# Cross-attention on folded weights in a four-layer Perceiver kernel, with context tiles, weights and normalisations prepared a stage earlier

## The reference, cut to what matters

```
x = x + L2_ffn(layernorm(x))      # 8 experts, top 2, 160 rows kept for each expert, relu
x = x + L3_xattn(layernorm(x), ctx_768, ...)
x = x + L3_attn(layernorm(x), ...)
x = x + L3_ffn(layernorm(x))      # 8 experts, top 2, no row dropped, gelu

def L3_xattn(m1, m2, ...):        # one head; the context has 257 rows of 192 features
    x1 = layernorm(m1, ln1_g, ln1_b);  x2 = layernorm(m2, ln2_g, ln2_b)
    q = x1 @ Wq + bq;  k = x2 @ Wk + bk;  v = x2 @ Wv + bv
    return softmax(q @ k.T * E ** -0.5) @ v @ Wo + bo

def L3_attn(x, ...):              # one head
    q, k, v = x @ Wq.T + bq, x @ Wk.T + bk, x @ Wv.T + bv
    qk = q @ k.T
    theta = 0.5 + 0.2 * sigmoid(qk) + 0.15 * tanh(qk) + 0.1 * relu(qk)
    return (softmax(theta) @ v) @ Wo.T + bo
```

## Time and profile before

| | |
|---|---|
| three runs | 1694.1 us median (1691.71 to 1694.96) |
| the profiled execution | 1691.59 us, span 1689.7 us |
| PE busy | 1527.2 us (90%) |
| DVE busy | 1060.3 us (63%) |
| ACT busy | 830.9 us (49%) |
| POOL busy | 767.7 us (45%) |
| mean granted TensorE clock | 0.96 |
| DMA | 204.52 MB, mean 121 GB/s |

### The profile page before, as it was taken

One profiled execution on the slowest core, in us unless ns is written; L12 is line 12 of the kernel. 1 busy time (PEld: TensorE's weight loads), 2 busy tenths in 40 slices (PEclk: granted clock), 3 DMA queues, 4 the chain that ended last, 5 costly groups with the idle time before them and its releaser, 6 DMA issues. The chain is left out here.

```text
span 1689.7 us, 37134 instructions
## 1 busy us (share of the span) xinstructions
PE 1527.2 (90%) x13507; PEld 1317.3 (78%) x13507; DVE 1060.3 (63%) x2934; ACT 830.9 (49%) x2414; POOL 767.7 (45%) x894
## 2 busy tenths in 40 slices
PE   7999999988888999988999999997769697859998
PEld 6899999856567999976899999964459644649997
DVE  5888888556867788865877777749831142353332
ACT  5766666555336787852766666640014122113332
POOL 7665666353339999943211211228823311113332
PEclk9999999999999999998999999999969988969999
DMA  8655554212013333303533333343056272942221
GB/s 259 199 165 175 172 165 150 99 70 83 1 39 101 132 134 132 134 22 102 187 110 111 130 108 108 126 162 100 0 168 182 45 239 90 360 144 33 39 39 26
DMA packets 127222, 204.52 MB, mean 121 GB/s; under 512 B 21034, under 2 KB 92363, under 8 KB 126659
## 3 DMA queue, kind: packets, MB, share of 16 engines
q1 hardware_dynamic: 119016, 188.83, 34.3%
q0 software_dynamic: 6720, 8.79, 3.2%
q10 hardware_dynamic: 1306, 4.51, 0.8%
HBM read 161.76 MB, written 41.14 MB: 120 GB/s over the span
## 5 line engine op out<-in xcount | busy, mean ns | idle before, releaser
L1074 DVE TENSOR_SCALAR xattn_oT<-banks,xattn_last 128x256 f32<-128x256 f32 x254 | 111.1, 479 | 89.8 <-PE banks L854 89.2
L963 ACT ACTIVATE xattn_probs<-banks,xattn_negmax 128x257 f32<-128x257 f32 x256 | 123.3, 482 | 85.4 <-DVE xattn_negmax L1055 85.2
L968 ACT ACTIVATE xattn_probs<-xattn_probs,xattn_rsum 128x257 f32<-128x257 f32 x256 | 131.3, 513 | 1.4 <-DVE xattn_rsum L1059 1.4
L1351 POOL TENSOR_SCALAR xattn_probs<-xattn_probs,xattn_rsum 128x257 f32<-128x257 f32 x128 | 119.4, 933 | 23.9 <-DVE xattn_rsum L1624 23.1
L974 ACT CAST xattn_probsT_hi<-banks 128x256 fp32r<-128x256 f32 x256 | 94.8, 370 | 57.2 <-PE banks L829 57.2
L1055 DVE TENSOR_REDUCE xattn_negmax<-banks 128x1 f32<-128x257 f32 x256 | 106.2, 415 | 13.4 <-PE banks L820 12.0
L1064 DVE TENSOR_TENSOR xattn_probsT_lo<-banks,xattn_probsT_hi 128x256 fp32r<-128x256 f32 x256 | 105.5, 412 | 11.2 <-ACT xattn_probsT_hi L974 10.2
L765 POOL COPY ctx_stat<-xattn_mv 128x2 f32<-128x2 f32 x32 | 6.0, 187 | 225.0 <-DVE xattn_mv L1088 225.0
L829 PE MATMUL banks<-ident,xattn_probs 128*128 128x128 f32 x512 | 101.6, 281 | 6.2 <-ACT xattn_probs L968 5.7
L816 PE MATMUL banks<-xattn_ctxT,xattn_qk_hi 128*128 128x258 f32 x256 | 93.7, 366 | 0.5 <-DVE xattn_qk L1051 0.5
L715 POOL TENSOR_SCALAR xattn_ctxT<-xattn_rawT 128x514 fp32r<-128x514 f32 x32 | 49.9, 1558 | 88.7 <-issue 82.5
(11 more groups left out here) (516 smaller groups left out, 5093.8 us busy)
## 6 DMA issues: line engine op xcount, KB each, us to landing
xattn_ctxT<-ctx_partsT SPq DMA_DIRECT2D x64, 516.0 KB, 4.1
xattn_ctxN<-ctx_partsN SPq DMA_DIRECT2D x64, 384.0 KB, 4.1
ctx_partsT<-xattn_ctxT SPq DMA_DIRECT2D x32, 516.0 KB, 2.7
moe_w<-in_L_ffn_W SPq DMA_DIRECT2D x16, 1024.0 KB, 12.8
ctx_partsN<-xattn_ctxN SPq DMA_DIRECT2D x32, 384.0 KB, 3.5
moecap_w_early<-in_L_ffn_w SPq DMA_DIRECT2D x10, 1024.0 KB, 10.3
xattn_rawN<-in_ctx SPq DMA_DIRECT2D x32, 192.0 KB, 2.7
...
```

The source lines that it names most:

```text
L963: nc.scalar.activation(probs[:, n % RING, :], SB[n % 2][:, 0:KV], ACT.Exp, bias=negmax[:, n % RING:n % RING + 1], accum_out=psum[:, n % RI ...
L968: nc.scalar.mul(probs[:, n % RING, :], probs[:, n % RING, :], rsum[:, n % RING:n % RING + 1]).then_inc(norm_ready, 1)
L1074: nc.vector.tensor_scalar(oT[k][:, heads, b, :], by_head(out_banks(n)[k][:, k * 2 * P:(k + 1) * 2 * P]), last[:, k, j * PER_TILE + b:j * P ...
L1351: nc.gpsimd.tensor_scalar(probs[:, n % RING, :], probs[:, n % RING, :], rsum[:, n % RING:n % RING + 1], None, ALU.mult).then_inc(norm_read ...
```

## The change

The parameters of the cross-attention are folded: once per run `m` is computed from Wq and Wk, `vo` from Wv and Wo, and the biases are folded alongside. This takes the place of `queries` and of `values`; `project(t)` is then two matmuls for each tile, in every step, and the walk has 12 steps. The folding itself is done by PE and ACT at the end of the capacity stage. Three context tiles of the cross-attention and all weights of the last attention are loaded by SP near the end of the capacity stage; the ring of context tiles has six places; the ring of experts' weights there has three, so that expert 3 and those after it are loaded when `down` of the expert three places earlier is done. The products of weights of the last attention, its folded biases and the first half of its layer norm are computed in the last four steps of the cross-attention; the last attention in turn starts the layer norm of the last expert stage. The tables and gate weights of the last expert stage are loaded a stage sooner, its experts 6 and 7 and its two bias arrays a stage later, behind the border.

```
+class SoftWeights:
+
+
+    LOADS = 8
...
+    def sp(self, sp):
+        for to, m in zip((self.wq, self.wk, self.wv, self.wo), self.drams):
+            sp.dma_start(to[:, :, :], m.rearrange("(c p) n -> p c n", p=P)).then_inc(self.loaded, 16)
+        for n in range(3):
+            sp.dma_start(self.b[:, n * CD:(n + 1) * CD], self.b_drams[n]).then_inc(self.loaded, 16)
+        sp.dma_start(self.bo[:, :], self.bo_dram.partition_broadcast(P)).then_inc(self.loaded, 16)
...
+    def queries_keys(self, pe, bank):
+        pe.wait_ge(self.loaded, 16 * self.LOADS)
+        self.product(bank, self.wq, self.wk).then_inc(self.qk_done, 1)
+
+    def values_out(self, pe, bank):
+        self.product(bank, self.wv, self.wo).then_inc(self.vo_done, 1)
...
+            pe.wait_ge(hw.qk_ready, 1)
             for n in range(2):
-                if soft_theta:
-                    pe.wait_ge(ln.xnT_ready, CD * (n + 1))
-                else:
-                    if n:
-                        ln.turn(pe, 1, LATE)
-                    ln.transposed(pe, n)
+                if n:
+                    ln.turn(pe, 1, LATE)
+                ln.transposed(pe, n)
...
+    RING = 3
...
-            for e in range(cw.EARLY + 1, E):
-                if e >= cw.RING:
-                    sp.wait_ge(down_done, e - cw.RING + 1)
+            for e in range(cw.RING, E):
+                sp.wait_ge(down_done, e - cw.RING + 1)
                 cw.load(sp, e)
+            for t in range(kv.EARLY):
+                kv.load_keys(sp, t)
+                kv.load_rows(sp, t)
+            hw.sp(sp)
...
+                if n == E:
+                    pe.wait_ge(hT_ready, E * FCH)
+                    xw.extra_columns(pe, EXTRA)
+                    xw.values_out(pe, VALUES_OUT)
+            xw.queries_keys(pe, QUERIES_KEYS, BIASES)
...
+            xw.take_extra_columns(act, EXTRA)
+            xw.take_values_out(act, VALUES_OUT)
+            xw.take_queries_keys(act, QUERIES_KEYS, BIASES)
             bring(act, range(1, TILES, 2))
...
         def _(sp):
-            gate.sp(sp)
-            sp.dma_start(token[:, :], d["token_number"]).then_inc(loaded, 16)
-            sp.dma_start(number[:, :], d["number"][0:BLOCKS].partition_broadcast(P)).then_inc(loaded, 16)
-            sp.dma_start(place[:, :], d["number"][1:P + 1].partition_broadcast(P)).then_inc(loaded, 16)
-            sp.dma_start(not_behind[:, :, :], d["not_behind"].partition_broadcast(P)).then_inc(loaded, 16)
-            sp.dma_start(spare[:, :], d["spare"][:, 0:BLOCKS]).then_inc(loaded, 16)
-            sp.dma_start(b1[:, :, :], d["L3_ffn_b1_cols"].rearrange("e p f -> p e f")).then_inc(loaded, 16)
-            sp.dma_start(b2[:, :, :], d["L3_ffn_b2"].partition_broadcast(P)).then_inc(loaded, 16)
+            ew.load(sp, ew.EARLY)
             rows.store(sp, ln, gate, stored, begun)
+            for e in range(ew.EARLY + 1, E):
+                ew.load(sp, e)
+            ew.biases(sp)
...
+    def values_out(self, pe, bank):
+        for of, out in ((slice(0, P), bank[:, 0:D]), (slice(P, self.CTX), bank[0:self.C2, D:2 * D])):
+            for k in range(CD):
+                mm = self.core.nc.tensor.matmul(out, self.wvT[:, k, of], self.wo[:, k, :], start=(k == 0), stop=(k == CD - 1))
+        mm.then_inc(self.vo_done, 1)
...
+    def queries_keys(self, pe, m_bank, b_bank):
+        nc, AUG, K2 = self.core.nc, self.AUG, self.AUG - P
+        pe.wait_ge(self.extra_ready, 2 * CD)
+        pe.wait_ge(self.wide_ready, 3)
+        for c in range(CD):
+            for k in range(CD):
+                nc.tensor.matmul(m_bank[:, c * AUG:(c + 1) * AUG], self.wqT[:, k, c * P:(c + 1) * P], self.wkT[:, k, :],
+                                 start=(k == 0), stop=(k == CD - 1))
+        for of, out in ((slice(0, P), b_bank[:, 0:1]), (slice(P, AUG), b_bank[0:K2, 1:2])):
+            for k in range(CD):
+                nc.tensor.matmul(out, self.wkT[:, k, of], self.bq[:, k:k + 1], start=(k == 0), stop=(k == CD - 1))
+        for k in range(CD):
+            nc.tensor.matmul(b_bank[:, D:2 * D], self.bv_wide[:, k, :], self.wo[:, k, :], start=(k == 0), stop=False)
+        nc.tensor.matmul(b_bank[:, D:2 * D], self.core.ident[:, :], self.bo[:, :], start=False, stop=True).then_inc(self.m_done, 1)
...
+            def project(t):
+                pe.wait_ge(oT_ready, 2 * (t + 1))
+                if t >= 2:
+                    pe.wait_ge(x_done, t - 1)
+                nc.tensor.matmul(Y[t % 2][:, 0:D], oT1[:, t % 2, :], vo1[:, :], start=True, stop=False)
+                nc.tensor.matmul(Y[t % 2][:, 0:D], oT2[:, t % 2, :], vo2[:, :], start=False, stop=True).then_inc(y_done, 1)
...
+            xw.folded(pe)
+            for h in range(2):
+                ln.pe(pe, h)
+                to_context(h)
+            for s in range(STEPS):
                 if s < TILES:
-                    if s < 2:
-                        pe.wait_ge(xT_ready, 2 * CD)
                     scores(s)
-                if s == 0:
-                    queries(1)
-                if s == 1:
-                    to_context(1)
                 if 0 <= s - 1 < TILES:
                     turn_probs(s - 1)
                 if 0 <= s - 3 < TILES:
                     turn_out(s - 3)
-                if s >= 5 and s % 2:
-                    values((s - 5) // 2)
-                if s >= 6 and s % 2 == 0:
-                    project((s - 6) // 2)
+                if 0 <= s - 4 < TILES:
+                    project(s - 4)
                 if 0 <= s - 2 < TILES:
                     probs_ctx(s - 2)
+                if s == QUERIES_KEYS_AT:
+                    pe.wait_ge(scaled_ready, TILES - 1)
+                    hw.queries_keys(pe, QUERIES_KEYS)
+                elif s == FOLD_AT:
+                    pe.wait_ge(scaled_ready, TILES)
+                    hw.fold_biases(pe, FOLD)
+                elif s == VALUES_OUT_AT:
+                    pe.wait_ge(probsT_ready, 2 * TILES)
+                    hw.values_out(pe, VALUES_OUT)
+                elif s == TURN_NEXT_AT:
+                    pe.wait_ge(o_ready, TILES)
+                    nx.turn(pe, 0, NEXT)
...
+                oh = soft_weights(core, until_attn3, ctx)
+                kv = ContextTiles(core, until_kv, ctx, cn)
+                stage_moe_capacity(core, cw, xw, kv, oh)
+            stage_xattn3(core, cn, xw, kv, to_attn3, oh)
+            until_kv.close()
         ew = ExpertWeights(core, ctx)
-        stage_attn3(core, ew)
-        stage_moe(core, ew)
+        stage_attn3(core, oh, to_attn3, to_moe, ew)
+        until_attn3.close()
+        stage_moe(core, ew, to_moe)
...
```

612 lines of the change are left out of this document (306 added, 306 removed).

## The result

The changed kernel takes 1665.5 us in the median of four executions (1659.9 to 1673.1), beside 1693.2 us (1691.7 to 1695.0) for the kernel before. The ratio is 0.985, with a 95% interval of 0.982 to 0.988. The profiled execution took 1663.99 us, its span is 1662.1 us.

A forecast was written before the change was run, and what follows sets the result against it. The prediction took chains of dependent work at stage starts and ends as the bound; 1.7 - 17.3 - 10.1 - 5.7 + 0.7 = -30.7 us from 1691.6 made 1660.9, forecast as 1662 us, range 1653 to 1671.

The forecast's parts named there:

- three signs: Wrong if `up` of experts 3 to 7 waits for DMA, `bring` starts over 3 us late, or first block awaits weights.
- Capacity stage, +1.7: End of the capacity stage: folding matmuls between last `down` and last `turn_y` cost 2.55 us, partly hidden by a 0.77 wait.
- Cost 0: Capacity stage: expert loads through the ring of three, and 23 transfers (5.8 MB) ahead of `bring`, were costed at 0.
- rival of the starving ring: Capacity stage: landings of 15.5 us make five experts wait 6.2 us each, 31 together, giving 1693 us; chance 0.03.
- rival of loads in their way: Capacity stage: loads slow the last experts' additions, giving 1665 us, or keep `bring` waiting, 1668 to 1676; chance 0.12.
- Folding behind `turn_y` at nothing: Capacity stage: about 3.8 us on PE and four ACT copies fit before `bring`, so cost nothing.
- Cross-attention, -17.3: Cross-attention: earlier start, first `turn_probs` at 22.7 us, and full steps of 3.9 us shorten the stage by 17.3 us.
- Pricing the second product by its gap: Cross-attention start: after a 1.5 us PE gap the second product runs at slow clock, 5.3 us instead of 3.7.
- A stretch at half clock in the walk, 0.17: Rival, cross-attention walk: one half-clock stretch costs 5.0 us, giving 1667 us, two 1672; chance 0.17.
- Last attention, -10.1: Last attention: takes 37.4 us where 47.5 stood, starting like the other one-head attention, without waiting for weights.
- Start of the last stage, -5.7 + 0.7: Last expert stage: first gate operation at 9.7 us instead of 15.5 (-5.7), late last expert and biases +0.7.
- late biases: Last expert stage: last expert and biases land 16.1 us after the first gate operation, costing 0.7, between 0 and 4.

The follow-up runs named there:

- after_again: The changed kernel run again with no edit, for a second profile: 1668.5 us, ratio 0.988 to the kernel before.
- no_early_tiles: Changed kernel with no context tile loaded before the cross-attention, six asked for at its start: 1676.4 us, ratio 0.995 to the kernel before.
- ring_of_four: Changed kernel with a fourth place for experts' weights, expert 3 loaded at once, two early tiles instead of three: 1664.1 us, ratio 0.985 to the kernel before.
- weights_in_walk: Changed kernel with the loads of the last attention's weights moved into the cross-attention: 1670.4 us, ratio 0.989 to the kernel before.
- experts_ahead: Changed kernel with all sixteen expert transfers of the last stage issued ahead of its border: 1671.1 us, ratio 0.989 to the kernel before.
- best: Changed kernel with four places for experts' weights, two early tiles, folding behind last `turn_y`, ACT's `bring` earlier, 78 small matmuls around last stage's start: 1667.7 us.
- fold_behind: Changed kernel with the whole folding moved behind the last `turn_y`: 1667.6 us, ratio 0.988 to the kernel before.

## Why the prediction was right, and where it was wrong

The forecast was 1662 us with a range of 1653 to 1671; 1665.5 was measured, and 1668.5 and 1668.3 in the two repetitions. The direction and the mechanism, chains taken out at three stage starts, hold. The working said -30.7 us. The changed part gave -24.5, -25.8 and -14.4 us in the three profiles. Of the three signs by which the prediction would call itself wrong, two came: `up` of experts 5 and 7 waited for DMA, and `bring` started 5.9 us later in its stage (120.3 for 114.4), not 3. Term by term:

- *Capacity stage, +1.7.* Measured +5.4. The folding's mechanism was right, its size 0.7 us too small: 3.2 us of matmuls for a wait of 0.77. **The step that failed is "Cost 0" for the loads.** The ring of three was costed at nothing with "1.6 us or more to spare, five times over". The 5.1 and 7.7 us behind that are the two transfers of one expert (issued at 1277.09 and 1277.50); for the second expert that the prediction names the trace has no landing. As the second transfer is issued 0.4 us behind the first, it left 1.2 us and not 1.6. In the changed kernel the two transfers for expert 5, issued at 1291.55 and 1291.96, landed after 5.1 and 9.7 us, and `up` of experts 5 and 7 began 0.82 and 0.33 us late. That is the mechanism of the rival of the starving ring, at a small size. And the additions were held for some 3 us by the tiles: the rival of loads in their way came true and belonged into the sum. I had given it 0.12 for want of a row with an addition beside full load; the rows of after_again are such rows, 7.8 us to landing for 3.2. no_early_tiles shows that the tiles are the cause, ring_of_four that two of them, asked for some 10 us sooner, cost nothing; weights_in_walk shows that the other loads are at most a small part. The half-clock stretch near the stage's start was shorter in the first profile than in the kernel before; where it was equal, the stage took +5.8 and +6.9.
- *Folding behind `turn_y` at nothing.* Right: ACT's copies ended at 1344.4, five us ahead of `bring`.
- *Cross-attention, -17.3.* Measured -16.5 and -16.0 where no half clock fell into the walk. The start was 1.4 us better than worked out (21.3 for 22.7), since the second product ran at full clock; a full step is 4.04 us for 3.9. The working said of the tiles only that no wait was left; no_early_tiles shows that the three early ones carry it. Pricing the second product by its gap was wrong: behind a gap of 1.54 us it took 3.70 us in all twelve profiles looked at (all of the table but the one before). It was the first product, behind 1.89 us, that varied: 3.70 us in ring_of_four and experts_ahead, 5.26 or 5.40 in the others. The Trainium skill ("TensorE: Matmul & The Clock Gate", section "What's actually happening") says that where the clock changes differs from run to run. The three profiles of the changed kernel agree at the end of the walk, where the clock fell in one of them and not in the two others.
- *A stretch at half clock in the walk, 0.17.* Too rare and too cheap. It was in one of three profiles of the changed kernel, at 7.5 us, and in four more kernels of the study whose walk never waited for tiles (ring_of_four, best, and shorter ones in fold_behind and experts_ahead): 5 of 11 profiles, some 1.5 to 7.5 us each by the length of the cross-attention. It can be part of the spread of 13 us between executions; the profiles are too few to say how much.
- *Last attention, -10.1.* Measured -8.9, -10.3 and -8.2. SP was through ahead of the border, as said; experts_ahead shows what it costs if it is not.
- *Start of the last stage, -5.7 + 0.7.* Measured -4.6 and +0.8 (+0.3 and +0.5 in the repetitions). The gate came at 10.9 us for 9.7: transposes and their copy took 2.2 us and not 1.5, and the answer of PE reached DVE 0.5 us behind the last logits and not 0.2. The late biases cost what was estimated; the last of them was issued at 1473.25 and landed 10.7 us later, at 1484.0, 17.8 us behind the gate.

The runs' -25.7 us by the ratio (-20.7 to -30.8) contain some us that no term has: the part ahead of the change lasted from 1228.0 to 1236.7 us in the profiles of the study, with the kernel before at 1232.2. Between the two profiled executions of the result 3.1 us of the gain lie ahead of the change. So the forecast of 1662 us came nearer to the time of the profiled execution (2 us) than its sum of -30.7 us came to the changed part's -24.5 (6 us); that much of its nearness is luck.
